# Attention denominators inverted in compact form once per four heads, with the heads passing DRAM and normalised four at a time

## The chip, the cores and the metric

The kernel runs on one core of a Trainium2 chip. The metric is the device time of one execution in microseconds. Five engines work side by side, each through its own instructions in order: TensorE (PE, with weight loads as PEld), VectorE (DVE), ScalarE (ACT), GpSimd (POOL) and SyncE (SP), which here issues every DMA.

## The reference

Two rows of 1024 tokens of width 512 pass six layers: half-weighted FFN 0, attention 0, FFN 0, FFN 1, attention 1, FFN 1, each behind a layer norm and added to its input. Only the attention layers are touched. Cut to the part that matters:

```python
att = jnp.einsum('bhqd,bhkd->bhqk', q, k) / scale      # 16 heads of 32, t = 1024, causal
att = jax.nn.softmax(att, axis=-1)
y = jnp.einsum('bhqt,bhtd->bhqd', att, v)
y = y.transpose(0, 2, 1, 3).reshape(b, t, n)
return y @ Wo.T + bo
```

The kernel leaves the softmax undivided until after the product with `v`: it computes a numerator `y` and a denominator per query, and multiplies by the inverse.

## The kernel before

`STAGES` lists the six layers; the attentions are stages 1 (`a0`, tiles `s1a0...`) and 4 (`a1`, tiles `s4a1...`). Each has 2 x 16 = 32 heads, worked in 8 groups of `HPG` = 4, groups 0 to 3 for the first batch row and 4 to 7 for the second. `make_plan` writes one list of steps and every engine's program walks it in that order, taking its own part of each step, so the list fixes the order on every engine and on SP's queue. Nothing overtakes.

A unit is one head and one key tile of 128: unit u is head u // 8, tile u % 8, and a group is 32 units. In unit u the plan puts, in this order: the steps due in jobs that run beside (`side.tick(0)`), the row maxima `row` for the unit 13 ahead (`AHEAD`: L1130 on PE, L1501 on DVE), the transposed scores `key` (L1148 on PE, exponentials L1335 on ACT), masking and pair sums on POOL (L1660, L1671), every second unit the products `pv` and `den` of units 9 back (L1167, L1178 on PE), and last the DMAs `stack` (L1745) that lay out q (and k) of the next group's heads: head 0's at unit 18 of the group, the others at 20, 26 and 31. The first `row` of the next group is in unit 19, and waits for head 0's stack. In attention 0 a k stack is needed once in four groups, in attention 1 in each.

PSUM holds for a head one bank of 128 x 512: on the partitions four quarters of the queries by 32 channels, in columns 0 to 255 the numerators, in columns 256 to 511 the denominators, each repeated over its 32 partitions. `times_v` starts a job when a head's last product is placed. For the last head of group g that is unit 7 of group g + 1, and the steps follow (units of group g + 1):

- 8: `y_fin`, on DVE a reciprocal of 128 x 256 (L1540) and a multiplication into `ysb` (L1544). It also frees the PSUM bank.
- 11: `y_move`, on SP four DMAs of 32 partitions (L1764) that bring the head from `ysb` into its 32 partitions of `y`.
- 14 and 15: `y_hi` (ACT, L1343) and `y_lo` (DVE, L1554), which split the group's `y` of 128 x 1024 into two parts in `yT`.
- 17 to 24: `oproj`, one token tile in each unit (PE, L1049), with `x_sum` (DVE, L1568) one unit behind.

The weights of the output projection of the next `oproj` come at unit 23 (`w_in`, SP) and are split at unit 24 on ACT (`w_split`, L1237) and POOL (L1635); the split waits for the last `oproj` of the group before, since it writes over its weights. Other weights of the next groups are loaded at units 17 and 19. `m_lo` (SP, L1755, units 5, 13, 21, 29) brings a head's maxima to its q stack, for its keys three units later. `bank_turns` gives the PSUM banks out by an estimate of when each comes free.

Of the kernel before, what the change touches and what calls it, by code (L numbers as in the profile page):

```python
# [17 lines left out]
P = 128  # L18
# [36 lines left out]
YT_AT = 2  # L55
O_LAG = 1
# [27 lines left out]
def into_heads(s):  # L84
    return s + 1 < len(STAGES) and not is_ffn(s + 1)

# [50 lines left out]
def make_plan():  # L137
# [112 lines left out]
    def attention(s, left):  # L250
# [71 lines left out]
        for g in range(GROUPS_ALL):  # L322
# [6 lines left out]
            put([split(s, "o", g, 0)], at + O_W_AT, 0)  # L329
# [18 lines left out]
        def times_v(n, jt):  # L348
# [5 lines left out]
            if k == PAIRS - 1:  # L354
                job = [[]] * Y_AT + [[("y_fin", s, n)]] + [[]] * Y_WAIT + [[("y_move", s, n)]]
                g, j = divmod(n, HPG)
                if j == HPG - 1:
                    job += [[]] * YT_AT + [[("y_hi", s, g)]] + [[("y_lo", s, g)]] + [[]] * O_LAG
                    job += timed(*((O_STEP * t, ("oproj", s, g, t)) for t in range(ST)),
                                 *((O_STEP * t + X_AFTER, ("x_sum", s, g, t)) for t in range(ST)))  # L360
                side.start(job)
# [65 lines left out]
    "e_add": ("e_add",), "den": ("den",), "y_fin": ("y_rec", "y_fin"),  # L427
# [59 lines left out]
class Pace:  # L487
# [10 lines left out]
    def run(self, step, banks):  # L498
# [84 lines left out]
        elif kind == "y_fin":  # L583
            done[step] = work("dve", 0.9, ("pv", s, where[0], ST - 1))
        elif kind == "y_hi":
            done[step] = work("act", 1.1, ("y_fin", s, (where[0] + 1) * HPG - 1))
# [9 lines left out]
def bank_turns(plan):  # L596
# [5 lines left out]
    for step in plan:  # L602
        width = banks_wanted(step)
        needs = []
        if width:
# [13 lines left out]
            if step[0] == "pv":  # L619
                release["y_fin", step[1], step[2]] = mine  # L620
# [44 lines left out]
def build(nc, a, out):  # L665
# [6 lines left out]
    with ExitStack() as ctx:  # L672
# [17 lines left out]
        moved = [ctx.enter_context(nc.semaphore(f"moved{i}")) for i in range(2)]  # L690
        stored = ctx.enter_context(nc.semaphore("stored"))
# [26 lines left out]
        for s, kind in enumerate(STAGES):  # L718
            t = T[s] = {}
            with ExitStack() as sc:  # L720
# [47 lines left out]
                else:  # L768
# [20 lines left out]
                    t["rden"] = [sbuf(sc, f"{tag}rden{i}", [P, QUAD]) for i in range(2)]  # L789
                    t["ysb"] = [sbuf(sc, f"{tag}ysb{i}", [P, QUAD]) for i in range(2)]  # L790
# [125 lines left out]

        def quarters_of(y):
            return y[:].rearrange("p (c t q) -> p t c q", c=HPG, q=HD)
# [49 lines left out]
        def read_by(step, k):  # L968

            kind = step[0]  # L970
            if kind == "pv":
                return sem["y_fin"], at("y_fin", "y_fin", *step[1:3])
# [225 lines left out]
        def scalar_program(act):  # L1198
# [138 lines left out]

            def y_hi(s, g):
                for n in range((g + 1) * HPG - 2, (g + 1) * HPG):
                    on.wait_ge(*y_moved(s, n))  # L1340
                if g:
                    on.wait_ge(sem["o_proj"], at("o_proj", "oproj", s, g - 1, ST - 1))
                act.activation(by_quarter(T[s]["yT"][HI]), quarters_of(T[s]["y"]),  # L1343
# [4 lines left out]
                     "key": key, "y_hi": y_hi}  # L1348
# [500 lines left out]
```

## Time and profile before

| | us |
|---|---|
| Median of three runs (lowest, highest) | 2633.96 (2629.57, 2639.21) |
| Span of the profiled execution | 2632.3 |
| PE busy in it | 2535.4 (96%) |
| DVE busy | 1533.2 (58%) |
| ACT busy | 1035.6 (39%) |
| POOL busy | 981.6 (37%) |

Attention 0 takes up about 320 to 780 us of the span, attention 1 about 1600 to 2095 us. The figures of whole engines mix these with four FFN layers, in which PE hardly ever rests, so the attentions are read by windows. Busy time on PE is modelled at the ends of its matmuls and can hide short waits.

### The profile page before, as it was taken

To read this page: it belongs to the slowest core of one execution; us is meant where nothing else is said; L and a number is where in the kernel's file an instruction comes from. 1 tells how busy PE (TensorE), PEld (TensorE's weight loads), DVE (VectorE), ACT (ScalarE), POOL (GpSimd) and SP (SyncE) were. 2 spreads that over 40 slices of the span, in tenths; PEclk is the share of its full clock that TensorE was granted. 3 is DMA by queue.
4 is the path that set the end of the run, shared out by engine and by line. 5 is a ranking of instruction groups with operands and counts; after the bars stand their busy time and mean duration, and the time that the engine had idled before them with its cause. 6 is when DMAs were issued, how large, how long until landed. Compare 5 with 4: busy or idle time off the path is not lost.

```text
span 2632.3 us, 44135 instructions
## 1 busy us (share of the span) xinstructions
PE 2535.4 (96%) x16928; PEld 2013.0 (76%) x16928; DVE 1533.2 (58%) x3356; ACT 1035.6 (39%) x1885; POOL 981.6 (37%) x1373
## 2 busy tenths in 40 slices
PE   6999989999999999999999999999999999999999
PEld 4788867667668888888888878677776678888887
DVE  7777579979975445433333345798589643333333
ACT  6555346656653223311111133566466431111111
POOL 5333566666643225211111122666366521111110
PEclk9999989999999999999999999999999999999999
DMA  4222131222220110100000002343233100000001
GB/s 148 73 73 73 39 76 46 51 68 64 48 93 1 36 45 12 37 25 25 24 25 25 25 17 58 92 94 75 52 88 79 37 32 25 24 25 25 25 17 64
DMA packets 72002, 128.73 MB, mean 49 GB/s; under 512 B 15728, under 2 KB 24944, under 8 KB 71792
## 3 DMA queue, kind: packets, MB, share of 16 engines
q1 hardware_dynamic: 71792, 125.92, 17.3%
q8 instruction: 134, 2.20, 0.4%
q14 instruction: 76, 0.62, 0.1%
HBM read 62.42 MB, written 13.63 MB: 29 GB/s over the span
## 4 chain that ended last, share of the span: by engine, by line
PE 81%; DVE 6%; POOL 2%; ACT 2%; SPq 2%; issue 2%; DMA 1%; DVEq 0%; ACTq 0%; POOLq 0%
PE psum L1049 65%; PE psum L1167 5%; PE psum L1130 4%; PE psum L1148 4%; PE psum L1178 2%; DVE psum L1501 2%; SPq L1745 1%; PE psum L1058 1%; DVE s1a0rden L1540 1%; ACT s1a0e L1335 1%; SPq L1764 0%; POOL s1a0e L1671 0%; ACT s4a1e L1335 0%; PE psum L1137 0%; POOL rstd L1610 0%
## 5 line engine op out<-in xcount | busy, mean ns | idle before, releaser
L1501 DVE CUSTOM_DVE_ANT_0 psum<-psum,mask_q 128x512 f32<-128x512 f32 (+5 forms) x768 | 413.2, 574 | 101.2 <-PE psum L1130 97.3
L1049 PE MATMUL psum<-hA_hi,wmem 128*128 128x256 f32 (+1 forms) x1536 | 405.2, 334 | 0.5 <-DVE s1a0negmax L1501 0.3
L1049 PEld LDWEIGHTS psum<-hA_hi,wmem 128*128 128x128 f32 x1536 | 270.3, 190 | 31.8 <-DVE s1a0negmax L1501 1.5
L1049 PE MATMUL psum<-hA_lo,wmem 128*128 128x512 f32 (+1 forms) x864 | 293.8, 340 | 0.0
L1335 ACT ACTIVATE s4a1e<-psum,p_scale 128x384 f32<-128x384 f32 (+5 forms) x384 | 205.5, 581 | 95.2 <-PE psum L1148 91.8
L1335 ACT ACTIVATE s1a0e<-psum,p_scale 128x384 f32<-128x384 f32 (+5 forms) x384 | 202.4, 578 | 78.1 <-PE psum L1148 76.8
L1454 DVE SCALAR_TENSOR_TENSOR x<-psum,x 128x512 f32<-128x512 f32 x256 | 175.7, 689 | 97.4 <-PE psum L1049 93.9
L1425 DVE TENSOR_TENSOR s5f1prod<-psum,s5f1silu 128x512 f32<-128x512 f32 x64 | 44.2, 691 | 303.7 <-PE psum L1049 303.7
L1425 DVE TENSOR_TENSOR s3f1prod<-psum,s3f1silu 128x512 f32<-128x512 f32 x64 | 44.2, 691 | 294.2 <-PE psum L1049 294.2
L1635 POOL TENSOR_TENSOR wmem<-raw,wmem 128x512 fp32r<-128x512 f32 x58 | 74.3, 1290 | 315.7 <-ACT wmem L1237 315.7
L1049 PE MATMUL psum<-s3f1w,s3f1a 128*128 128x512 f32 x768 | 181.6, 390 | 0.9 <-POOL s3f1w L1635 0.9
L1049 PE MATMUL psum<-s5f1w,s5f1a 128*128 128x512 f32 x768 | 180.0, 390 | 1.6 <-POOL s5f1w L1635 1.6
L1049 PEld LDWEIGHTS psum<-hA_lo,wmem 128*128 128x128 f32 x864 | 164.8, 191 | 19.8
L1671 POOL TENSOR_TENSOR s4a1e<-s4a1e 128x896 f32<-128x896 f32 (+3 forms) x128 | 164.8, 1288 | 17.4 <-ACT s4a1e L1335 6.4
L1671 POOL TENSOR_TENSOR s1a0e<-s1a0e 128x896 f32<-128x896 f32 (+3 forms) x128 | 164.6, 1286 | 17.1 <-ACT s1a0e L1335 5.8
L1049 PEld LDWEIGHTS psum<-s5f1w,s5f1a 128*128 128x128 f32 x768 | 143.9, 188 | 32.3 <-issue 2.0
L1049 PEld LDWEIGHTS psum<-s3f1w,s3f1a 128*128 128x128 f32 x768 | 143.5, 188 | 31.1 <-DVE s3f1prod L1425 1.1
L1645 POOL TENSOR_TENSOR x<-x,s0f0dso 128x512 f32<-128x512 f32 x64 | 89.0, 1412 | 136.1 <-DVE s0f0dso L1449 136.1
L1660 POOL TENSOR_SCALAR_AFFINE_SELECT s4a1e<-s4a1e 128x128 f32<-128x128 f32 x256 | 74.9, 299 | 166.6 <-ACT s4a1e L1335 164.9
L1635 POOL TENSOR_TENSOR s5f1w<-raw,s5f1w 128x512 fp32r<-128x512 f32 x32 | 40.8, 1296 | 242.4 <-ACT s5f1w L1237 242.4
L1635 POOL TENSOR_TENSOR s3f1w<-raw,s3f1w 128x512 fp32r<-128x512 f32 x32 | 40.8, 1295 | 241.4 <-ACT s3f1w L1237 241.4
L1148 PE MATMUL psum<-s1a0qst,s1a0kst 98*128 98x384 f32 (+4 forms) x384 | 118.1, 362 | 12.9 <-ACT s1a0e L1335 7.8
(195 smaller groups left out, 5581.8 us busy)
## 6 DMA issues: line engine op xcount, KB each, us to landing
s1a0qst<-s1a0qs SPq DMA_DIRECT2D x96, 128.0 KB, 2.3
s4a1qst<-s4a1qs SPq DMA_DIRECT2D x96, 128.0 KB, 2.4
s4a1kst<-s4a1ks SPq DMA_DIRECT2D x96, 128.0 KB, 2.4
raw<-in_gate SPq DMA_DIRECT2D x44, 256.0 KB, 2.9
raw<-in_up SPq DMA_DIRECT2D x44, 256.0 KB, 2.8
raw<-in_down SPq DMA_DIRECT2D x44, 256.0 KB, 2.8
rounded<-s0f0w SPq DMA_DIRECT2D x24, 256.0 KB, 2.0
s2f0w<-rounded SPq DMA_DIRECT2D x24, 256.0 KB, 4.9
```

The lines of the kernel that those rows point to most:

```text
L1049: ins = pe.matmul(out_, w, m, start=n == 0, stop=n == len(terms) - 1)
L1130: pe.matmul(ps[:, 0, 0:pw], q_st[0:STACK, j, i * P:(i + 1) * P], k_st[0:STACK, j, z * pw:(z + 1) * pw], start=True, stop=True).then_inc(se ...
L1148: pe.matmul(ps[:, 0, 0:pw], k_st[0:STACK + 2, j, jt * P:(jt + 1) * P], q_st[0:STACK + 2, j, q0 + z * pw:q0 + (z + 1) * pw], start=True, st ...
L1167: ins = pe.matmul(psum[c * HD:(c + 1) * HD, bank, jt * HD:QUAD], v[:, jt, kv, :], e[:, :, c, :], start=jt == 0, stop=jt == ST - 1, skip_gr ...
L1335: act.activation(T[s]["e32"][:, begin_ + z * pw:begin_ + (z + 1) * pw - skip], src, ACT.Exp, bias=p_scale[:]).then_inc(sem["exp"], 1)
L1425: dve.tensor_tensor(prod[:], psum[:, bank, :], silu[:], ALU.mult).then_inc(sem["prod"], 1)
L1454: dve.scalar_tensor_tensor(x[:, tile, :], src, 0.5, x[:, tile, :], ALU.mult, ALU.add).then_inc(sem["x_add"], 1)
L1501: dve.tensor_tensor_reduce(scores, scores, mask_q[:, first:first + pw], -1.0, -MASKED, ALU.add, ALU.min, T[s]["negmax"][n % 2][:, column:c ...
L1635: pool.tensor_tensor(lo, buf[:], hi.bitcast(F32), ALU.subtract).then_inc(sem["w_lo"], 1)
L1645: pool.tensor_tensor(x[:, tile, :], x[:, tile, :], T[s]["dso"][nth(*step) % 2][:], ALU.add).then_inc(sem["x_pool"], 1)
L1660: pool.affine_select(out=block, in_=block, compare_op=ALU.is_ge, fill=0.0, base=0, pattern=[[1, P]], channel_multiplier=-1).then_inc(sem[" ...
L1671: pool.tensor_tensor(e32[:, begin + P:end], e32[:, begin + P:end], e32[:, more:more_end], ALU.add).then_inc(sem["e_add"], 1)
```

## The change

For all groups but the last of each attention (`in_place`), the head is no longer inverted and multiplied in PSUM. ACT copies the whole bank of 128 x 512 into a larger `ysb` (`y_out`). One DMA stores it in DRAM (`y_save`, 256 KB), one loads the numerators back into `y` (`y_load`, 128 KB). Once in four heads, `den_in` reads the denominators without repetition, 4 x 1024 numbers laid out as 128 x 32; DVE inverts these (`y_rec`), `y_keep` stores them in DRAM, `y_spread` reads them back repeated over 32 partitions per head (128 x 1024, 512 KB) into `spread`, which shares memory with the high part of `yT`, and DVE multiplies the group's `y` by it (`y_norm`). The last group of each attention keeps the old way. The units of group g + 1 in which the steps stand:

| step | engine | before | after |
|---|---|---|---|
| y_fin / y_out | DVE / ACT | 8 | 8 |
| y_move / y_save | SP | 11 | 10 |
| y_load of heads 0 to 2 (ahead of y_save) | SP | - | 10 |
| y_load of head 3, den_in | SP | - | 13 |
| y_rec | DVE | - | 15 |
| y_keep | SP | - | 16 |
| y_spread | SP | - | 18 |
| y_norm | DVE | - | 22 |
| y_hi, y_lo | ACT, DVE | 14, 15 | 23, 24 |
| oproj | PE | 17 to 24 | 26 to 33 |
| x_sum | DVE | 18 to 25 | 27 to 34 |
| w_in, w_split of the next oproj | SP, ACT and POOL | 23, 24 | 35, 36 |

Units 33 and up lie in the next group. The heads' own `y_save` stand in units 2, 10, 18 and 26. Core of the diff:

```diff
+SAVE_WAIT = 1
+LOAD_WAIT = 2
+REC_AT, KEEP_AT, SPREAD_AT, NORM_AT = 2, 3, 5, 9
+def in_place(g):
+    return g == GROUPS_ALL - 1
...
-            put([split(s, "o", g, 0)], at + O_W_AT, 0)
+            if g == 0:
+                put([split(s, "o", g, 0)], at + O_W_AT, 0)
...
+                else:
+                    job = [[]] * Y_AT + [[("y_out", s, n)]] + [[]] * SAVE_WAIT
+                    job += [[("y_load", s, m) for m in range(n - j, n) if j == HPG - 1]
+                            + [("y_save", s, n)]]
+                    job += [[]] * LOAD_WAIT
                 if j == HPG - 1:
-                    job += [[]] * YT_AT + [[("y_hi", s, g)]] + [[("y_lo", s, g)]] + [[]] * O_LAG
+                    if not in_place(g):
+                        job += timed((0, ("y_load", s, n)), (0, ("den_in", s, g)),
+                                     (REC_AT, ("y_rec", s, g)), (KEEP_AT, ("y_keep", s, g)),
+                                     (SPREAD_AT, ("y_spread", s, g)), (NORM_AT, ("y_norm", s, g)))
+                    job += [[("y_hi", s, g)]] + [[("y_lo", s, g)]] + [[]] * O_LAG
...
+            def y_out(s, n):
+                if n >= 2:
+                    on.wait_ge(*ysb_left(s, n - 2))
+                on.wait_ge(sem["pv"], at("pv", "pv", s, n, ST - 1))
+                act.activation(T[s]["ysb"][n % 2][:], psum[:, banks["pv", s, n, 0][0], :],
+                               ACT.Copy).then_inc(sem["y_out"], 1)
...
+            def y_rec(s, g):
+                on.wait_ge(den_loaded, 16 * (nth("y_rec", s, g) + 1))
+                dve.reciprocal(T[s]["rden"][:], T[s]["den"][:]).then_inc(sem["y_rec"], 1)
+            def y_norm(s, g):
+                on.wait_ge(y_loaded, HPG * 16 * (nth("y_norm", s, g) + 1))
+                on.wait_ge(rden_spread, 16 * (nth("y_norm", s, g) + 1))
+                y = T[s]["y"]
+                dve.tensor_tensor(y[:], y[:], T[s]["spread"], ALU.mult).then_inc(sem["y_norm"], 1)
...
+            def y_load(s, n):
+                g, j = divmod(n, HPG)
+                on.wait_ge(*y_saved(s, n))
...
+            def y_keep(s, g):
+                k = nth("y_keep", s, g)
+                on.wait_ge(sem["y_rec"], at("y_rec", "y_rec", s, g))
...
+            def y_spread(s, g):
+                k = nth("y_spread", s, g)
+                on.wait_ge(rden_kept, 16 * (k + 1))
...
+                sp.dma_start(T[s]["spread"], rdens[k % 2].unsqueeze(1).broadcast_to([HPG, HD, SEQ])
+                             ).then_inc(rden_spread, 16)
```

## Rows read from the trace of the kernel before

**Rows 1.** Busy time by windows, both attentions (columns: PE, PEld, DVE, ACT, POOL, clock, DMA).

```profile
365.00:769.00 404.00, 378.49 (x4375) 274.38 (x4372) 356.17 (x985) 244.03 (x481) 282.73 (x445) 0.99 0.24 58
...
1645.00:2083.00 438.00, 417.62 (x4654) 313.87 (x4653) 355.13 (x972) 257.93 (x507) 271.86 (x436) 0.99 0.32 76
```

**Rows 2.** Same view, single groups, cut at unit 13: attention 0, then attention 1.

```profile
412.40:460.60 48.20, 46.97 (x557) 34.68 (x555) 45.46 (x129) 29.55 (x59) 32.65 (x51) 1.00 0.24 57
460.60:521.70 61.10, 55.16 (x601) 39.54 (x601) 56.40 (x156) 39.96 (x77) 42.57 (x75) 1.00 0.20 50
521.70:588.00 66.30, 60.23 (x626) 45.08 (x624) 50.85 (x138) 32.53 (x67) 43.94 (x60) 0.97 0.29 66
...
685.00:739.90 54.90, 49.59 (x542) 33.41 (x541) 51.31 (x146) 37.43 (x70) 39.81 (x74) 0.97 0.25 60
...
1696.00:1749.80 53.80, 52.65 (x606) 40.70 (x605) 47.21 (x132) 32.27 (x64) 33.29 (x52) 1.00 0.36 85
1749.80:1810.60 60.80, 56.71 (x626) 42.30 (x625) 54.33 (x151) 41.31 (x79) 42.37 (x76) 1.00 0.32 76
1810.60:1890.40 79.80, 76.66 (x714) 60.22 (x713) 47.23 (x135) 34.59 (x69) 33.38 (x52) 1.00 0.24 58
...
1997.20:2053.70 56.50, 52.30 (x566) 35.41 (x565) 53.45 (x147) 39.06 (x74) 41.31 (x75) 0.97 0.34 81
```

**Rows 3.** Chain of waits at unit 24 of group 1, attention 0 (start us, us, what).

```profile
430.53 0.37 ACT s1a0ow L1237
```

**Rows 4.** Groups of ACT instructions in attention 0, shapes apart.

```profile
L1229 ACT ACTIVATE hA_hi<-psum 128x512 fp32r<-128x512 f32 x16 | 9.5, 593 | 0.0
...
L1237 ACT ACTIVATE s1a0ow<-raw 128x512 fp32r<-128x512 f32 x8 | 5.1, 632 | 9.2 <-PE psum L1049 4.9 <-DMA raw<-in_o 4.3
```

**Rows 5.** Groups of DVE instructions, shapes apart: busy us, mean ns | idle before.

```profile
L1540 DVE RECIPROCAL s1a0rden<-psum 128x256 f32<-128x256 f32 x32 | 55.9, 1745 | 6.4 <-PE psum L1167 6.4
...
L1544 DVE TENSOR_TENSOR s1a0ysb<-psum,s1a0rden 128x256 f32<-128x256 f32 x32 | 13.6, 424 | 2.2
...
L1554 DVE TENSOR_TENSOR s1a0yT<-s1a0y,s1a0yT 128x1024 fp32r<-128x1024 f32 x8 | 9.9, 1234 | 1.6 <-ACT s1a0yT L1343 1.6
```

**Rows 6.** Timeline of ACT at a head's first unit, attention 0 [idle before <-releaser].

```profile
440.53 1.27 ACT L1335 ACTIVATE s1a0e<-psum,p_scale 128x512 f32<-128x512 f32 x2 [0.66 <-PE psum L1148]
```

**Rows 7.** Page, part 6: DMA issues, KB each, median us from issue to landing.

```profile
s1a0qst<-s1a0qs SPq DMA_DIRECT2D x96, 128.0 KB, 2.3
...
rounded<-s0f0w SPq DMA_DIRECT2D x24, 256.0 KB, 2.0
...
s1a0y<-s1a0ysb SPq DMA_DIRECT2D x128, 32.0 KB, 1.8
...
s1a0ropek<-in_rope SPq DMA_DIRECT2D x1, 512.0 KB, 4.2
```

**Rows 8.** Issues on SP of one line: min/median/max ns each.

```profile
L1745 SPq DMA_DIRECT2D s1a0qst<-s1a0qs x96: 507/590/1575, 324.6 to 721.6; - x96
```

**Rows 9.** Timeline, group 1 of attention 0, units 15 and 19 (start us, us, what).

```profile
414.06 0.62 PE L1130 MATMUL psum<-s1a0kst,s1a0qst 96*128 96x512 f32 x2
...
415.10 1.21 DVE L1554 TENSOR_TENSOR s1a0yT<-s1a0y,s1a0yT 128x1024 fp32r<-128x1024 f32 x1
...
421.21 0.40 PE L1130 MATMUL psum<-s1a0kst,s1a0qst 96*128 96x512 f32 x1
```

**Rows 10.** Timeline, group 0 of attention 0, the same rows, without output projections.

```profile
367.65 0.64 PE L1130 MATMUL psum<-s1a0kst,s1a0qst 96*128 96x512 f32 x2
...
372.63 0.40 PE L1130 MATMUL psum<-s1a0kst,s1a0qst 96*128 96x512 f32 x1
```

**Rows 11.** Timeline, group 1 of attention 1, units 15 and 19.

```profile
1700.38 1.22 DVE L1554 TENSOR_TENSOR s4a1yT<-s4a1y,s4a1yT 128x1024 fp32r<-128x1024 f32 x1
...
1700.81 0.63 PE L1130 MATMUL psum<-s4a1kst,s4a1qst 96*128 96x512 f32 x2
...
1708.10 0.47 PE L1130 MATMUL psum<-s4a1kst,s4a1qst 96*128 96x512 f32 x1 [0.56 <-DMA s4a1kst<-s4a1ks]
```

More of the change, by code:

```diff
@@ L583, in run @@
         elif kind == "y_fin":
-            done[step] = work("dve", 0.9, ("pv", s, where[0], ST - 1))
+            done["y", s, where[0]] = done[step] = work("dve", 2.2, ("pv", s, where[0], ST - 1))
+        elif kind == "y_out":
+            done["y", s, where[0]] = done[step] = work("act", 0.68, ("pv", s, where[0], ST - 1))
+        elif kind == "y_rec":
+            work("dve", 0.35)
+        elif kind == "y_norm":
+            work("dve", 1.25)
         elif kind == "y_hi":
-            done[step] = work("act", 1.1, ("y_fin", s, (where[0] + 1) * HPG - 1))
+            done[step] = work("act", 1.1, ("y", s, (where[0] + 1) * HPG - 1))
         elif kind == "y_lo":
@@ L690, in build @@
         moved = [ctx.enter_context(nc.semaphore(f"moved{i}")) for i in range(2)]
+        saved = [ctx.enter_context(nc.semaphore(f"saved{i}")) for i in range(2)]
+        y_loaded = ctx.enter_context(nc.semaphore("y_loaded"))
+        den_loaded = ctx.enter_context(nc.semaphore("den_loaded"))
+        rden_kept = ctx.enter_context(nc.semaphore("rden_kept"))
+        rden_spread = ctx.enter_context(nc.semaphore("rden_spread"))
+        heads_out = nc.dram_tensor("heads_out", (2, HPG, P, CH), F32, kind="Internal").ap()
+        rdens = nc.dram_tensor("rdens", (2, HPG, SEQ), F32, kind="Internal").ap()
         stored = ctx.enter_context(nc.semaphore("stored"))
@@ L915, in y_moved, with y_saved, ysb_left, y_whole @@
             return moved[n % 2], HPG * 16 * (nth("y_move", s, n) // 2 + 1)
+        def y_saved(s, n):
+            return saved[n % 2], 16 * (nth("y_save", s, n) // 2 + 1)
+        def ysb_left(s, n):
+            return y_moved(s, n) if in_place(n // HPG) else y_saved(s, n)
+        def y_whole(s, g):
+            if in_place(g):
+                return [y_moved(s, n) for n in range((g + 1) * HPG - 2, (g + 1) * HPG)]
+            return [(sem["y_norm"], at("y_norm", "y_norm", s, g))]
         def quarters_of(y):
@@ L971, in read_by @@
             if kind == "pv":
[L972 removed]
+                name = "y_fin" if in_place(step[2] // HPG) else "y_out"
+                return sem[name], at(name, name, *step[1:3])
             if kind == "piece":
@@ L1769, in sync_program @@
+            steps = {"begin": begin, "open": open_, "y_move": y_move, "y_save": y_save, "y_load": y_load, "den_in": den_in,
+                     "y_keep": y_keep, "y_spread": y_spread, "x_in": x_in_, "w_in": w_in, "w_keep": w_keep,
                      "w_back": w_back, "stack": stack, "m_lo": m_lo}
```

66 lines of the change are left out of this document (47 added, 19 removed).

## The prediction

> **What bounds the kernel now.** The busy times of the whole span mix the attentions with four FFN layers, so I cut the span at the attentions, the only layers touched, and read busy time by windows. In attention 0 PE is busy 378.5 of 404.0 us and DVE 356.2; in attention 1 it is 417.6 of 438.0 and 355.1 [rows 1]. PE therefore rests 25.5 + 20.4 = 45.9 us in both. That is the ceiling of any gain, since the change takes no matmul away, and it matters more than the DVE time that is saved.
>
> Next I cut by groups [rows 2]. Two kinds show. In an ordinary group PE rests 48.2 - 47.0 = 1.2 us (attention 0) or 53.8 - 52.7 = 1.1 us (attention 1); groups 4 and 5 repeat these. Groups 2 and 6 carry layer norms and group 3 the turn to the other batch row. There PE rests 5.9, 6.1 and 5.3 us in attention 0, and 4.1, 3.1 and 4.2 us in attention 1, together 28.7 us, with DVE at 56.4 of 61.1 and 51.3 of 54.9 us. So DVE limits three groups in eight; in the rest PE is full.
>
> The chain of waits tells what the 1.2 us of an ordinary group are. At unit 24 ACT splits the weights of the output projection only after the last projection of the group before; the exponentials behind it come late, and PE waits for a bank: 0.37 us of the split stands on the chain itself [rows 3], with an exponential behind it. ACT's idle time ahead of these splits, 4.9 us, has PE as releaser [rows 4].
>
> **DVE's part.** 56 of the 64 heads lose 1.745 + 0.424 = 2.17 us each [rows 5], 121.5 us. 14 groups gain a reciprocal of 32 columns instead of 256, 1.745 / 8 = 0.22 us (up to 0.3 with a start-up cost), and a product of 128 x 1024, for which the nearest row is the subtraction of that shape, 1.23 us [rows 5]. That is 14 x 1.5 = 21 us. DVE is relieved of 100 us, but PE gets back at most its rest. Of the 28.7 us in groups 2, 3 and 6 I take 60%, 17 us (between 8 and 26: ACT and the DMAs of these groups hold a part). In the six ordinary groups the split moves to unit 36, two units behind the last projection, which cures that wait: 6 x 1.1 = 6.5 us. Relief: 23.5 us, at most 35 us.
>
> **ACT's part.** 56 copies of a bank, 0.593 us each by the copy of that shape [rows 4], 33 us of ACT. ACT is busy 244 of 404 and 258 of 438 us [rows 1], so time is there, but the copy stands at unit 8 of each head's count, just ahead of the two longest exponentials, behind a wait for the head's last product. Queued behind it are the exponentials that free PE's banks. ACT rests 0.66 us at such a place now, waiting for PE [rows 6], and the bank of the head itself comes free 1.6 us earlier (0.6 instead of 2.17). I take 0.1 us a head, 5 us; the bounds are 0 (all in the gap, or a little below by the earlier bank) and 33 us.
>
> **SP's part, and the wait that is new.** Four issues a head become two, plus three a group; issues get fewer, yet three of the new ones wait for a DMA to land or for DVE, and SP's queue stands still behind them. I follow which waiter matters.
>
> `y_load` and `den_in` wait for `y_save` to land. From the end of the last product: 0.6 copy, 2.0 store (the 256 KB store [rows 7]), two issues, about 2.2 for the load: 6 us. `y_rec` is seven units later, 8.7 us at PE's pace of 5.0 us for four units [rows 10] (these are the heavy units, so rather less). It is just in time, and the maxima of unit 13 behind it on SP aren't due before. I cost this at nothing; if the cover goes, DVE waits and all below moves out by the same time.
>
> The pair `y_keep`, `y_spread` is another matter. `y_spread` stands in unit 18 and a unit's jobs come ahead of its stacks. So the q stack of the next group's first head, in unit 18 too, and PE's first `row` on it, unit 19, stand behind: DVE reaching `y_rec`, its end, the landing of `y_keep`, the issue of `y_spread`, the issue of `y_save`, and only then the stack's own issues and landing. PE is in order, so everything waits with that `row`.
>
> In time, for attention 0: `y_rec` stands where `y_lo` stood, 415.10 in group 1 [rows 9]. Then 0.3 (reciprocal) + 1.9 (between 1.8 of the small DMA and 2.0 of a store to DRAM [rows 7]) + 0.5 + 0.5 (two issues at the shortest [rows 8]) + 1.2 + 2.3 (two more issues at the median [rows 8], and the landing of the stack's third from its issue [rows 7]) = 6.7 us, so the stack is there at 421.8. When does PE want it? Before, at 421.21, but three output projections lay between, and they now stand from unit 26 on. Group 0 has no projections and shows PE's own pace: 372.63 - 367.65 = 5.0 us from the `row` of unit 15 to that of unit 19 [rows 10]. From 414.06 [rows 9] this gives 419.1. Stall: 2.7 us. In attention 1 a k stack follows, three issues or 1.8 us more: 1700.38 + 8.5 = 1708.9, wanted at 1700.81 + 5.0 = 1705.8 [rows 11]; the stall is 3.1 us. The wait of 0.56 us that is there now [rows 11] goes off it: 2.5 us.
>
> To this comes that the 512 KB of `y_spread` and the 256 KB of `y_save` travel just ahead of the stack. A 512 KB load took 4.2 us against 2.3 for 128 KB [rows 7]. The surplus of 1.9 us is a bound, as most of it runs while SP still issues; I take 0.9 us. So 3.6 and 3.4 us, or 3.5 in each ordinary group: 6 x 3.5 = 21 us. In groups 2, 3 and 6 of both attentions the stall falls partly into rest that is there anyway, and I take half: 6 x 1.75 = 10.5 us. Group 0 has no `y_spread` in it, group 7 no stack. Sum 31.5 us. Bounds: 12 x 0 if something else holds PE or DVE reaches unit 15 much sooner, 12 x (3.1 + 1.9) = 60 us.
>
> Where a page bears on it: the rows show 1.8 to 2.0 us for DMAs of 32 KB as of 256 KB [rows 7]. The Trainium skill, "DMA: Bandwidth & Descriptors", in its anatomy of one DMA, puts a fixed cost of some 2.0 us on each and says that it is mostly the receipt of the write, which can take long when the target is HBM. With that 2.0 for each landing, `y_keep` costs 0.1 us more, 12 x 0.1 = 1 us. The same page asks for pieces of 512 bytes or more; `den_in` and `y_keep` move pieces of 128 bytes, and no row before shows a store of this kind. The trace agrees as to the fixed cost.
>
> **Late projections.** They fill units 26 to 33 instead of 17 to 24. PE's work is the same. The groups' q and k pieces lie in units 0 to 14, so only the last two projections meet them. At the end of a stage the projection of group 6 runs out of the loop by two tiles, and the last group's weights follow it while the last head is still inverted and moved; I cost that at nothing, 1 us a stage if not covered.
>
> **Sum.** 31.5 + 5 - 23.5 = +13 us. Against the span of the profiled execution, 2632.3 us, which is 1.7 us under the median of the runs and well inside their spread, this is 2645.3, rounded to 2645 us.
>
> **Rivals.**
>
> - The stack is not late (faster). If DVE, freed of its backlog, reaches `y_rec` a unit or two earlier relative to PE, or PE is slowed in units 15 to 19 by the copies on ACT so that it doesn't want the stack sooner, the stall is gone and only relief is left: 2632.3 - 23.5 + 5 = 2614 us, down to 2600 with the upper relief. Against it: DVE's slot in group 0 and 1 lies just one microsecond behind PE's `row`, so there is hardly a backlog to lose; for it, that in groups 2 and 6 DVE does lag.
> - Both cancel (same). Stalls at half my size, 16 us, or relief of 35 us: 2632.3 + 16 + 5 - 23.5 = 2630 us, to 2636.
> - ACT becomes the limit at head starts (slower still). With 0.6 us per head on PE's path, 33 instead of 5 us: 2645 + 28 = 2673 us. It decides from the point where ACT's rest ahead of unit 8 is below the copy; the idle time of ACT at large speaks against it.
> - The change doesn't do what it says: if the loads kept DVE waiting at `y_rec` or `y_norm`, DVE would stand while its rows are due and lose what it was given; 14 groups x 2 us on top of the forecast give 2673 us. Part of the slower case.
>
> **How the numbers follow.** The forecast, between 2638 and 2660, has 0.45. The faster rival has 0.22, the cancelling one 0.23, the two worse ones together 0.10. A measurement of this kernel can tell about 0.3% or 8 us from no change, 2626 to 2642. Of the forecast's 0.45 some 0.07 lie under 2642, and the upper edge of the faster rival and the lower of the cancelling one meet at 2626. So faster 0.21, same 0.31, slower 0.48. The range leaves out the lower half of the faster rival and the worst of the slow ones: 2614 to 2668 us.
>
> **What would show it.** In the changed profile, the `row` instructions of PE (scores for the maxima) that follow a new stack should wait 3 us for the DMA of the q stack in attention 0 and the k stack in attention 1, twelve times, 30 us or more in sum. On SP the q stack should start right behind `y_spread`, some 3 us after the small reciprocal. DVE should be busy about 100 us less over both attentions, and ACT 33 us more. The wait of the output weights' split for the projection should be gone. The prediction is wrong if these `row` waits sum to under 15 us, or if PE's rest in groups 2, 3 and 6 shrinks by much more than 17 us.

## The result and the profile after

The changed kernel takes 2800.7 us in the median (2798.2 to 2802.1) against 2636.6 for the kernel before beside it. The ratio is 1.0626, with a 95% interval of 1.0607 to 1.0645: 164 us slower, where 13 had been forecast. The sign was right, the size was wrong by a factor of twelve, and the time lies far outside the range of 2614 to 2668 us.

The head of the page of the kernel after (span; busy time and share of each engine):

```profile
span 2798.2 us, 43919 instructions
...
PE 2567.1 (92%) x16928; PEld 2034.9 (73%) x16928; DVE 1466.8 (52%) x3272; ACT 1059.9 (38%) x1941; POOL 995.5 (36%) x1373
```

Two sums can be read from it. PE rests 2798.2 - 2567.1 = 231.1 us, and 2632.3 - 2535.4 = 96.9 before, so 134.2 us more. And PE is busy 31.7 us longer with the same 16928 matmuls. The two make up the whole difference of the spans, 165.9 us. The second one says that the same matmuls took longer.

Who makes PE rest stands in the waits of PE (who waited for what: us in total, times, longest). L1182 is `row` (L1130 before), L1200 is `key`:

```profile
PE psum L1182 <- DMA s4a1kst<-s4a1ks: 78.5, 7, 13.8
PE psum L1182 <- DMA s1a0qst<-s1a0qs: 49.1, 5, 11.9
...
PE psum L1200 <- DMA s1a0qst<-s1a0mrow: 13.9, 4, 10.3
PE psum L1182 <- DMA s1a0kst<-s1a0ks: 13.7, 2, 11.6
PE psum L1200 <- DMA s4a1qst<-s4a1mrow: 10.3, 3, 9.6
```

The first row of scores of a group waits for its stack 14 times, 78.5 + 49.1 + 13.7 = 141.3 us. Two of these stacks have no broadcast ahead of them (2.1 and 3.4 us). The other twelve are the place which the prediction named: 135.8 us, or 11.3 us a time, where 3.5 us in an ordinary group and 31.5 us in all had been forecast. None of the twelve is under 8.2 us, so the half that the prediction took off in groups 2, 3 and 6 isn't there either. The two `mrow` lines (a head's maxima on their way into its q stack) have a single wait of some 10 us in each attention, which was not foreseen at all.

One such wait, group 1 of attention 0. SyncE's timeline there (start, us, line, transfer):

```profile
415.35 0.35 SPq L1864 DMA_DIRECT2D rdens<-s1a0den  x1
415.75 0.43 SPq L1789 DMA_DIRECT2D raw<-in_q  x1
416.80 0.59 SPq L1872 DMA_DIRECT2D s1a0yT<-rdens  x1
417.45 0.46 SPq L1839 DMA_DIRECT2D heads_out<-s1a0ysb  x1
418.02 3.74 SPq L1811 DMA_DIRECT2D s1a0qst<-s1a0qs  x6
```

and the chain of waits through it:

```profile
415.12 0.22 DVE s1a0den L1607
415.35 1.43 DMA rdens<-s1a0den
416.80 0.59 SPq L1872
...
417.45 0.46 SPq L1839
...
419.27 9.05 DMA s1a0qst<-s1a0qs
...
428.46 0.77 PE psum L1182
```

The order and the times of the issues are those of the prediction almost to the tenth: `y_rec` at 415.12 (predicted 415.10), the stack's second issue ended at 419.2 (419.5 by the forecast). Then the landing takes 9.05 us instead of 2.3.

Why, the busy time by windows shows (us; PE, PEld, DVE, ACT, POOL; then the granted clock, the share of the 16 DMA engines that is busy, GB/s):

```profile
418.00:420.00 2.00, 0.70 (x3) 0.38 (x3) 1.58 (x3) 1.37 (x4) 1.82 (x1) 1.00 0.79 237
420.00:422.00 2.00, 0.00 (x0) 0.00 (x0) 0.28 (x1) 0.30 (x1) 1.73 (x3) 1.00 1.00 213
422.00:424.00 2.00, 0.00 (x0) 0.00 (x0) 0.00 (x0) 0.00 (x0) 0.00 (x0) 0.73 0.68 129
424.00:426.00 2.00, 0.00 (x0) 0.00 (x0) 0.00 (x0) 0.00 (x0) 0.00 (x0) 0.50 0.25 100
426.00:428.00 2.00, 0.00 (x0) 0.00 (x0) 0.00 (x0) 0.00 (x0) 0.00 (x0) 0.50 0.26 98
428.00:430.00 2.00, 1.54 (x7) 1.03 (x11) 0.63 (x2) 0.41 (x1) 0.00 (x0) 0.50 0.05 14
430.00:432.00 2.00, 2.00 (x26) 1.13 (x19) 0.13 (x2) 0.53 (x2) 1.67 (x2) 0.50 0.00 0
```

Two things are to be seen. From 424 to 428 a quarter of the DMA engines is busy, 4 of 16, at 100 GB/s. Under way are the broadcast `y_spread`, issued 7 us before, and the last parts of the stack; I read this as the broadcast on four engines, with the stack's share queued behind it, and test it below. And the granted clock: it is 1.00 while PE begins to rest, falls to 0.50 (1.2 of 2.4 GHz), and stays there until 432 at least, so PE's first microseconds of work after the rest run at half speed. The first `row` at 428.46 takes 0.77 us; before, at the full clock, it took 0.40 [rows 9]. That is where the same matmuls take longer.

Single instructions took about what was forecast. The `y_norm` takes 1.21 and 1.32 us (forecast 1.23), the small reciprocal 0.34 (0.22 to 0.3). The wait of the output weights' split for the projection, 4.9 and 5.0 us before, is gone. The copy on ScalarE, from the groups of ACT by shape, takes what the row of its shape said [rows 4]:

```profile
L1394 ACT ACTIVATE s1a0ysb<-psum 128x512 f32<-128x512 f32 x28 | 16.6, 593 | 1.8 <-PE psum L1219 1.6
```

But VectorE is busy only 66 us less over the span, where 100 had been forecast. 23 of the 34 missing stand in 64 small instructions that the change doesn't touch, the minima of 128 x 4 (L1510 before, L1569 after): 35.6 us before, 58.7 after. One of them, from the timelines of VectorE and GpSimd:

```profile
384.85 2.05 DVE L1569 TENSOR_TENSOR s1a0negmax<-s1a0negmax 128x4 f32<-128x4 f32 x1
384.79 2.09 POOL L1737 TENSOR_TENSOR s1a0e<-s1a0e 128x896 f32<-128x896 f32 x1
```

Alone such an instruction takes 0.16 us. Each one that takes more than 0.4 us, 29 of 64 before and 52 after, began while a GpSimd TENSOR_TENSOR was under way and ended within 0.04 us of its end. So VectorE stands there until GpSimd is done, and after the change it comes to that place more often while GpSimd works. Part of the relief is lost that way.

### The profile page after: what moved, and what is told of

Read it like the earlier page. It is cut to its first block, busy times and chain, and to the rows that moved or that the text cites. A ratio compares the mean times of both kernels' runs of the same rounds, so it can differ in the third digit from the quotient of the medians.

```text
span 2798.2 us, 43919 instructions
## 1 busy us (share of the span) xinstructions
PE 2567.1 (92%) x16928; PEld 2034.9 (73%) x16928; DVE 1466.8 (52%) x3272; ACT 1059.9 (38%) x1941; POOL 995.5 (36%) x1373
## 4 chain that ended last, share of the span: by engine, by line
PE 80%; DMA 6%; DVE 4%; SPq 2%; issue 1%; ACT 1%; POOL 1%; DVEq 0%; ACTq 0%; POOLq 0%
PE psum L1101 63%; PE psum L1182 5%; PE psum L1219 5%; PE psum L1200 4%; DMA s4a1kst<-s4a1ks 2%; PE psum L1230 2%; DMA s1a0qst<-s1a0qs 2%; DVE psum L1560 1%; SPq L1811 1%; PE psum L1110 1%; DMA s1a0kst<-s1a0ks 0%; PE psum L1189 0%; DMA rdens<-s4a1den 0%; DMA rdens<-s1a0den 0%; DVE stats L1426 0%
## 5 line engine op out<-in xcount | busy, mean ns | idle before, releaser
L1182 PE MATMUL psum<-s4a1kst,s4a1qst 96*128 96x512 f32 (+4 forms) x384 | 127.3, 390 | 79.6 <-DMA s4a1kst<-s4a1ks 78.5
L1182 PE MATMUL psum<-s1a0kst,s1a0qst 96*128 96x512 f32 (+4 forms) x384 | 129.1, 396 | 63.8 <-DMA s1a0qst<-s1a0qs 49.1
L1737 POOL TENSOR_TENSOR s4a1e<-s4a1e 128x896 f32<-128x896 f32 (+3 forms) x128 | 166.3, 1300 | 17.4 <-ACT s4a1e L1387 6.5
L1726 POOL TENSOR_SCALAR_AFFINE_SELECT s4a1e<-s4a1e 128x128 f32<-128x128 f32 x256 | 81.2, 320 | 244.0 <-ACT s4a1e L1387 242.9
L1726 POOL TENSOR_SCALAR_AFFINE_SELECT s1a0e<-s1a0e 128x128 f32<-128x128 f32 x256 | 82.0, 325 | 176.8 <-ACT s1a0e L1387 176.4
L1182 PEld LDWEIGHTS psum<-s4a1kst,s4a1qst 96*128 96x128 f32 x384 | 68.9, 199 | 102.8 <-issue 86.0
```

The costliest lines, as they stand in the source:

```text
L1182: pe.matmul(ps[:, 0, 0:pw], q_st[0:STACK, j, i * P:(i + 1) * P], k_st[0:STACK, j, z * pw:(z + 1) * pw], start=True, stop=True).then_inc(se ...
L1726: pool.affine_select(out=block, in_=block, compare_op=ALU.is_ge, fill=0.0, base=0, pattern=[[1, P]], channel_multiplier=-1).then_inc(sem[" ...
L1737: pool.tensor_tensor(e32[:, begin + P:end], e32[:, begin + P:end], e32[:, more:more_end], ALU.add).then_inc(sem["e_add"], 1)
```

## Experiments on the broadcast

The kernel before took 2636.1 to 2639.3 us beside them, so medians can be compared directly, but between experiments that were run at different times only to about 3 us. The interval in brackets is that of the ratio to the kernel before.

**The broadcast as four DMAs.** Its source is 4 heads x 32 repetitions x 1024. The experiment issues one DMA by head, whose outermost dimension is 32:

```diff
-sp.dma_start(T[s]["spread"], rdens[k % 2].unsqueeze(1).broadcast_to([HPG, HD, SEQ]))
+for j in range(HPG):
+    sp.dma_start(T[s]["spread"][j * HD:(j + 1) * HD, :],
+                 rdens[k % 2, j].unsqueeze(0).broadcast_to([HD, SEQ]))
```

> The changed kernel with one edit: the DMA that spreads the inverses over the partitions is issued as four DMAs of 32 partitions, so that the outermost dimension of each is 32 and not 4. Its place in the queue stays. Theory A (width): in the changed kernel the spread's 512 KB went over a quarter of the 16 DMA engines (busy share 0.25 and 0.26 from 424 to 428 us, 100 GB/s), and the stack behind it on these engines landed 9 us late. Spread over all engines it is gone in 2 to 3 us; the wait of PE's row for the stack shrinks from 8 to 12 us to about 3 or 4 us each, 141 us to about 45 us in sum, and the kernel takes 2640 to 2665 us. Theory B (place): the wait comes from the order alone (inversion, store, landing, spread, stack), whatever the width; then 2790 us or more remain. Theory C: reading one DRAM row 32 times is what is slow; then it stays above 2750 us too, with the busy share high on all 16 engines.

Measured: 2719.1 us (1.0284 to 1.0318), 82 us less. Windows at the same wait, after a first issue of the broadcast at 414.64:

```profile
416.00:418.00 2.00, 0.55 (x3) 0.23 (x2) 1.73 (x3) 1.51 (x3) 1.96 (x1) 1.00 0.85 247
418.00:420.00 2.00, 0.00 (x0) 0.00 (x0) 0.14 (x1) 0.06 (x1) 1.59 (x3) 0.85 0.86 263
420.00:422.00 2.00, 0.65 (x2) 0.59 (x3) 0.00 (x0) 0.00 (x0) 0.00 (x0) 0.50 0.93 209
422.00:424.00 2.00, 2.00 (x23) 1.18 (x25) 0.76 (x2) 0.95 (x2) 0.78 (x2) 0.50 0.15 31
```

The stretch at a quarter is gone, and with it theories B and C. The first rows of the groups wait 65.4 us for stacks instead of 141.3. The width was half of the loss, but theory A had 2640 to 2665 us and about 45 us of waits: 2719 is well above it, and the rest has other causes. The four DMAs also add three issues ahead of the stack: its first issue comes 3.73 us behind that of `y_keep`, and 2.64 in the changed kernel (medians of twelve groups). So by width alone the loss is rather more than 82 us.

**The broadcast behind the first stack** (`SPREAD_AT` 5 to 6; one DMA), and **both edits together**:

> The changed kernel with one edit: the spread, still one DMA, stands in unit 19 and so behind the stack of head 0 (unit 18) and ahead of the k weights and the stack of head 1 (unit 20). Theory A (width): stack 0 is no longer behind the slow transfer, but the stack of head 1 and the maxima of unit 21 are; head 1's row is only due at unit 27, some 8 us later, so most of the 9 us is covered. The row's wait for stack 0 all but goes (under 2 us each), about half of the 164 us or more comes back: 2640 to 2700 us. Theory B (place): with the spread out of the way the time falls to about that of the kernel before or below, 2620 to 2640 us, and splitting it in four on top adds nothing.

> Both edits: four DMAs, in unit 19. My sum had 31.5 us for the stalls at stack 0, 23.5 us of relief and 5 us for the copies on ACT. Without the stall 2614 us are to come out (2605 to 2630). If the relief of DVE and of the weights' split is worth nothing, 2637 us; if the copies on ACT cost 33 us, 2640 us or more. Against e1 the difference is the price of the place alone, once the width is cured: 20 to 40 us.

Measured: 2743.6 (1.0381 to 1.0415) and 2689.5 us (1.0171 to 1.0201). Both expectations were missed: theory A had 2640 to 2700 us for the first, and 2605 to 2630 had been expected of the second. The difference to the first experiment, 20 to 40 us by expectation, was met: the place ahead of the stack costs 30 us with the wide broadcast (57 with the narrow one). The width still costs 54 us where the broadcast stands behind the stack: `key` then waits for the maxima (18.3 and 10.9 us), and in attention 1 `row` waits for ScalarE's exponentials, 20.6 us in four waits, which I have not followed further.

**One DMA, but with an outermost dimension of 16.** The first experiment leaves open whether four DMAs help by being four. Here the reciprocals are kept four times over, so that one DMA can read 16 rows, each 8 times:

```diff
-rdens[k % 2].unsqueeze(1).broadcast_to([HPG, HD, SEQ])
+rdens[k % 2].rearrange("j r q -> (j r) q").unsqueeze(1).broadcast_to([HPG * HPG, HD // HPG, SEQ])
```

> The changed kernel (2800.7), the broadcast still one DMA of 512 KB to the same places, but the reciprocals are kept four times over, so that the outermost dimension of its source is 16 and not 4 (three small stores more by group). Theory (the outermost dimension of 4 leaves 12 of the 16 DMA engines out, and the stacks queue behind on the four): as with four DMAs of 32 partitions (2719), 2705 to 2730, and the stretch at a quarter of the DMA engines is gone. Rival (one DMA of 512 KB is slow by its size or by reading the same 4 KB again and again, and four DMAs were quicker for being four): 2785 or more.

Measured: 2752.0 us (1.0413 to 1.0453), between the two, and a miss: 2705 to 2730 had been expected. The trace shows both halves of that. Windows, then SyncE's timeline:

```profile
422.00:424.00 2.00, 0.00 (x0) 0.00 (x0) 0.00 (x0) 1.15 (x3) 1.51 (x2) 0.50 0.95 272
424.00:426.00 2.00, 0.00 (x0) 0.00 (x0) 0.00 (x0) 0.00 (x0) 0.00 (x0) 0.50 1.00 336
```

```profile
415.84 2.64 SPq L1865 DMA_DIRECT2D rdens<-s1a0den  x4
418.54 0.47 SPq L1789 DMA_DIRECT2D raw<-in_q  x1
419.91 0.61 SPq L1873 DMA_DIRECT2D s1a0yT<-rdens  x1
420.56 0.58 SPq L1839 DMA_DIRECT2D heads_out<-s1a0ysb  x1
421.25 3.77 SPq L1811 DMA_DIRECT2D s1a0qst<-s1a0qs  x6
```

All 16 engines are busy, at 336 GB/s (broadcast and stack together), no stretch at a quarter follows, and the one DMA lands in 4.9 us (median). So the outermost dimension is the cause, not the number of DMAs.

Why it isn't 2719: the four small stores occupy SyncE for 2.64 us instead of 0.35, so the stack's first issue comes 5.0 us behind that of the first store (median of twelve groups). With four broadcasts it is 3.73. The number of issues ahead of the stack is the same there, one store and four broadcasts against four stores and one broadcast, but those of the broadcasts are shorter (0.4 us against 0.55). That is 1.3 us a group, some 15 of the 33 us. The stack also lands later behind the one DMA, in 4.12 us instead of 3.04 in this group. Together the first rows wait 94.4 us for stacks instead of 65.4, 29 of the 33 us. My expectation had left these issues out.

The rule of the width could have been read beforehand. The Trainium skill, "DMA: Bandwidth & Descriptors", section "Why a DMA increments its semaphore by 16 and not by 1", says that a DMA runs on the largest number of engines up to 16 that divides the slowest dimension not of size 1 of its source and of its destination alike; for 4 and 128 that is 4. The trace agrees: 0.25 of the engines.

**No keep, no spread.** `y` is multiplied by itself, which leaves the normalisation out and its VectorE time in:

> The changed kernel without the store of the inverses and without their spread; the group's y is multiplied by itself at the same place, so that the output is not normalised. DVE and ACT do the same work as in the changed kernel, SP waits for no landing ahead of the stack, and 512 KB per group are not moved. It is the floor of what the change can give. By my terms 2614 us; by the theory that all of the loss is the spread, 2636 us or less; if the copies on ACT, the stores of the heads or the late projections cost much by themselves, it stays above 2650 us.

Measured: 2676.6 us (1.0127 to 1.0157). So keep and spread, wide and behind the stack, cost 13 us. Without them the kernel is still 1.4% slower than before, where my terms had 2614 us: something other than the inverses' way is wrong too.

## Experiments on VectorE's relief and the late projections

**The weights' split later, in the kernel before** (`O_W_AT` 23 to 26):

> The kernel before with one number changed: the split of the next group's output weights lies at unit 26 of a group instead of 23, so VectorE no longer stands waiting at it while the projection of the units before runs. This is one term of my sum by itself (the wait in front of the split, 6.5 us over the twelve groups, which I took as given back to TensorE). If the term is right: about 2633 against 2639.3. If VectorE's wait was off TensorE's path: 2639, within 2. If the split then comes too late for the projection that uses it, TensorE waits there and the time rises over 2645.

Measured: 2641.3 (1.0003 to 1.0022). Nothing is gained, against the 6 us of the expectation. PE's waits for the exponentials are 9.4 + 9.4 us in it, against 7.8 + 8.3 before. The expectation speaks of VectorE where the split is on ScalarE and GpSimd; the number is unaffected.

**The kernel before without the reciprocal, and then with ScalarE's copy in place of the whole normalisation.** In the second nothing of it is left on VectorE. Both leave out the true normalisation, and both change all 64 heads:

```diff
-dve.reciprocal(rden[:], psum[:, bank, QUAD:CH])
-dve.tensor_tensor(T[s]["ysb"][n % 2][:], psum[:, bank, 0:QUAD], rden[:], ALU.mult)
+act.activation(T[s]["ysb"][n % 2][:], psum[:, banks["pv", s, n, 0][0], :], ACT.Copy)
```

> The kernel before without the 56 reciprocals: the numerators are multiplied by ones, so the normalisation is left out, and the 1.7 us by head that the change wants to save are gone with nothing put in their place: no DMA, no copy by ScalarE, no later projection. It measures the relief of VectorE alone. My theory (it was the limit only in stretches of groups 2, 3 and 6): 17 us less, about 2622. Rival (VectorE was nowhere the limit, TensorE's share of 92% sets the time): within 3 of 2639. Second rival (it was the limit in every group): 2600 or less.

> The kernel before with the numerators leaving PSUM by a copy of ScalarE (128x512, numerators and denominators in one, as in the change) and nothing put on VectorE in its place; the normalisation is left out, the heads still go from chip to chip and the projections stay in their units. Against the kernel that left out the reciprocals alone (2628.7) it measures ScalarE's copy. My term: 5 us of TensorE's time, so about 2634 (bounds 0 to 33: 2629 to 2662). If the copy is what remains of the change when the spread is gone and the projections are back (2657), 2650 or more.

Measured: 2628.7 (0.9956 to 0.9980) and 2623.4 us (0.9934 to 0.9959). Taking the reciprocal away brings 7 to 8 us, where 17 had been expected. (The first expectation speaks of 56 reciprocals and of TensorE's share of 92%; the edit takes out 64, and 92% is the share in the changed kernel, 96% in the one before.) Taking the multiplication too and giving ScalarE the copy brings 5 more, where the copy was to cost 5. What the copy costs by itself isn't separated by this. The net relief is 14 us; 23.5 - 5 = 18.5 had been put down. It is what the change could have won if the inverses' way and the later order of work had cost nothing, and no run here was faster.

**The kernel before with late projections.** The halves of `y` nine units later, the split of the next output weights behind the projections, and the first head of a group moved behind the halves, so that SyncE doesn't stand there. Core of the edit:

```diff
-YT_AT = 2
+YT_AT = 11
-job = [[]] * Y_AT + [[("y_fin", s, n)]] + [[]] * Y_WAIT + [[("y_move", s, n)]]
+job = [[]] * Y_AT + [[("y_fin", s, n)]] + [[]] * (8 if g and j == 0 else Y_WAIT) + [[("y_move", s, n)]]
```

> The kernel before with the split of y and the projections later by nine units (y's two halves at units 22 and 23, the first projection at 25), the split of the next output weights behind them, and the first head of a group moved at unit 24, behind the halves, so that SyncE's queue doesn't stand there. Nothing else is changed: it is the step that I costed at nothing. Theory (the projections are the work that lies between the stacks' issue and the row of scores that reads them, and without them TensorE rests there and its clock falls): waits for the stacks grow from 8 to 30 us or more, 2655 to 2670. If my step was right: within 5 of 2636.

Measured: 2651.4 (1.0043 to 1.0071), 14 us more. PE's waits in it (L1133 is `row`):

```profile
PE psum L1133 <- DMA s4a1kst<-s4a1ks: 11.7, 7, 3.2
...
PE psum L1133 <- DMA s1a0kst<-s1a0ks: 6.2, 2, 4.0
```

They were 3.8 and 4.5 us before, so the projections did cover a part of the stacks' way. Moving them isn't free, as the prediction had it, and isn't the 19 us or more that I then expected of it.

> The kernel before with ScalarE's copy in place of the normalisation (2623.4) and with the late projections (2651.4) in one; the normalisation is left out. If the two terms are independent, 2637 (14 less, 14 more). If VectorE's relief is worth more where the projections are late, under 2633. The distance from here to the kernel without spread and with the saves behind the stacks is the price of the trips through DRAM themselves: I expect 0 to 6 us.

Measured: 2631.5 (0.9963 to 0.9985). Beside the copy on ScalarE, lateness costs 8 us and not 14. The terms aren't independent. The waits for the stacks are nearly the same (16.1 us against 17.9), and VectorE's share of the chain that ended last falls from 10% to 4%, so the gain is on VectorE's side; more than that isn't shown.

## Experiments on what was still open

**The tied head.** In group 7 heads go from `ysb` to `y` directly, as before. The first one's `y_move` (unit 19) overwrites `y`, so it waits for `y_lo` of group 6, which stood at unit 15 and now stands at 24. SyncE stands still at it, with the low half of the maxima queued behind. In the kernel with both edits (four DMAs, behind the stack), end of attention 0, the chain (L1613 is `y_norm`, L1402 and L1620 the halves, L1830 `y_move`, L1821 the maxima):

```profile
758.71 1.71 DVE s1a0y L1613
760.45 1.06 ACT s1a0yT L1402
761.53 1.46 DVE s1a0yT L1620
763.05 0.57 SPq L1830
...
765.57 0.69 SPq L1821
766.30 1.76 DMA s1a0qst<-s1a0mrow
768.20 1.94 PE psum L1200 x4
```

The experiment is the kernel with both edits and `Y_WAIT` 8 for that head alone:

> The kernel with the spread in four pieces and behind the first stack of the row (2689.5), with one number changed: in the group whose heads are moved to their place on the chip alone, the first head is moved at unit 25 and not at unit 19, so that SyncE's queue no longer stands at that move until the group before has been split into its two halves (unit 24), with the low half of the rotated keys queued behind. If the tie is what TensorE waits for at unit 24 of group 7 (8.1 us in each attention): 17 us less, about 2672. If the wait there has another cause, within 3 of 2689.

Measured: 2672.1 us (1.0123 to 1.0149), 17 less, as expected (13 by the ratios to the kernel before). The waits of `key` for the maxima were 10.9 and 9.2 us; 2.9 and 1.7 us are left. The maxima now go ahead of the moves:

```profile
761.78 1.32 SPq L1821 DMA_DIRECT2D s1a0qst<-s1a0mrow  x2
...
766.35 5.90 SPq L1830 DMA_DIRECT2D s1a0y<-s1a0ysb  x8
```

**Projections back in their units, without keep and spread** (`LOAD_WAIT` 2 to 0, `REC_AT` 1, `NORM_AT` 2):

> The kernel without the keep, the spread and the true reciprocals (the rows of y are multiplied by themselves; 2676.6), with the split of y and the projections back in the units in which the kernel before has them (14 to 24, instead of 23 on); loads and normalisation are moved earlier for it. Theory: the late projections no longer lie between the stacks' issue and the row of scores that reads them, and this costs some 30 us, and the tie at unit 24 of group 7 17 more, partly the same time: about 2620 to 2640. Rival (what is left over the kernel before comes from ScalarE's copies and the extra transfers): 2665 to 2680.

Measured: 2657.3 (1.0064 to 1.0091), 19 less than without that edit, of which the tie alone would be 17. Neither 2620 to 2640 nor the rival's 2665 to 2680 came out, and it was a poor experiment: it moved loads, product and projections at once, and PE waited 5.3 us in each attention for ScalarE's copies instead. It suggested, no more, that the late projections weren't what kept the time high.

**The saves ahead of the stacks.** The chain of the kernel without keep and spread, group 1 of attention 1:

```profile
1713.66 0.61 ACT s4a1ysb L1393
...
1714.29 0.34 SPq L1837
...
1714.74 0.56 SPq L1809
...
1719.37 2.40 DMA s4a1kst<-s4a1ks
...
1721.90 0.77 PE psum L1181
```

`y_save` (L1837) of the new group's first head stands one unit earlier than the `y_move` that it replaces, and thereby ahead of the stack and not behind it. It waits for ScalarE's copy, and the copy for the last product of the head. SyncE was done with the weights' load before it at 1709.14 + 0.44, and the stack's first issue comes at 1714.74, 5.2 us later. The experiment moves the saves of heads 0 and 1 one unit on, with the tied head moved later as well, once with the broadcast in four behind the stack, once without it:

```diff
-job = [[]] * Y_AT + [[("y_out", s, n)]] + [[]] * SAVE_WAIT
+job = [[]] * Y_AT + [[("y_out", s, n)]] + [[]] * (2 if j < 2 else SAVE_WAIT)
```

> The kernel with the broadcast in four, behind the stacks, and the tied head moved later (2672.1), with the saves of the first two heads of a group one unit later, so that they stand behind the stacks of units 18 and 26 in SyncE's queue and no longer ahead. Theory (the stacks wait behind a save that waits for ScalarE's copy): 15 to 22 us less, 2650 to 2657. Rival (the save costs nothing there, and what is left is the trips' traffic or the broadcast): within 4 of 2672.

> The kernel without keep, spread and true normalisation (2676.6), with the tied head moved later and the saves of the first two heads of a group behind the stacks. The tie alone gives 2659; with the saves' place right: 2637 to 2643. Rival (the saves cost nothing there): 2656 to 2662.

Measured: 2658.8 (1.0065 to 1.0099), 13 less than 2672.1 and a little short of the 15 to 22 expected, and 2639.9 us (1.0003 to 1.0026), 19 to 20 less than 2676.6 - 17.4 = 2659.2, as expected. SyncE's timeline without the broadcast:

```profile
1689.40 0.44 SPq L1787 DMA_DIRECT2D raw<-in_q  x1
1690.99 1.82 SPq L1809 DMA_DIRECT2D s4a1qst<-s4a1qs  x3
1694.73 2.32 SPq L1809 DMA_DIRECT2D s4a1kst<-s4a1ks  x3
1697.10 0.58 SPq L1837 DMA_DIRECT2D heads_out<-s4a1ysb  x1
```

The stack starts 1.2 us after the weights' load. Of the 22 us by which 2659.2 was over the kernel before, 19 are found. Between the late projections with ScalarE's copy (2631.5) and this kernel (2639.9) the trips through DRAM, the product of 128 x 1024, the small reciprocal and the old way of group 7 are left: 8 us, where 0 to 6 had been expected.

**All three mended, with one DMA whose source is 16 wide.**

> The changed kernel with all three mended: the source of the broadcast 16 wide, the broadcast behind the first stacks, and the first head of the last group moved at unit 25. It is the best form of the change in its own order of work. Sum of the single steps: 2672, as with four DMAs and the move later (2672.1); 2662 to 2682. If the steps don't add up so with one DMA, over 2690. By what is left (late projections, trips through DRAM, ScalarE's copy) it doesn't come below 2655, over the kernel before.

Measured: 2699.6 us (1.0217 to 1.0245), 27 over the same kernel with four DMAs and over the expected 2662 to 2682. The four stores hold the first stack up by 1.45 us a group in the mean, 17 us in twelve groups, and the first rows wait 66.7 us for stacks instead of 46.5; the rest of the 27 isn't shown. None of the versions with the whole normalisation beats the kernel before. The best, with the saves behind the stacks, is 0.8% over it: the relief is worth 14 us, and in every form tried the rest of the way through DRAM costs more than that.

## Why the prediction was wrong, step by step

The step that failed most is the 0.9 us a group (1.9 as its bound) that the prediction took for the bytes of `y_spread` and `y_save` ahead of the stack: the stack's landing took 9.05 us instead of 2.3. It had the place and the order right, and took the cost of the broadcast from its bytes. The late projections, put at nothing, cost 8 us; the tied head, which the prediction doesn't have, cost 17; and the issue of `y_save` was counted without the wait in it, 19.

One edit at a time, from the kernel before to the kernel after (each step is the difference of two medians, in this order; another order would share them out differently):

| step | us | predicted |
|---|---|---|
| the copy on ScalarE in place of the normalisation | -14 | -18.5 |
| projections and split late | +8 | 0 |
| trips through DRAM, product, small reciprocal | +8 | within the relief |
| saves ahead of the stacks (19 to 20) and the tied head (17) | +37 | 0.5 us a group for the save's issue; none for the tie |
| keep and spread, wide, behind the first stack | +13 | no term of its own |
| spread ahead of that stack | +30 | with the next, 31.5 |
| its width: 4 DMA engines instead of 16 | +82 | 0.9 us a group |

The steps of 8 us are known to about 3. The last row also holds what three fewer issues ahead of the stack give back; by 1.1 us a group, an estimate from the issue times above, the width alone would be some 95 us.

- *DVE's part and ACT's part* were of the right kind. The ceiling of PE's rest [rows 1, 2] held. The 6.5 us for the split [rows 3] were wrong: a wait that stands on the chain for 0.37 us is no proof that the time comes back when it goes (2641.3 us with the split later). VectorE was relieved of 66 us and not of 100; 23 of the missing 34 are the minima that stand behind GpSimd. ACT's term of 5 us doesn't show: the copy in place of the multiplication brought 5 us.
- *The wait that is new* was the right mechanism at the right place, and its issue times were right. PE wanted the stack when predicted too: it stops between 418 and 420, with 419.1 forecast. The term that failed is the surplus of 0.9 us for the 512 KB and 256 KB ahead of it, with 1.9 as a bound: the landing grew from 2.3 to 9.05 us. The bound came from a 512 KB load [rows 7] that has as many bytes but not the same pattern, and the pattern stood in the diff. The landing of `y_keep`, on the other hand, was put too long: 1.9 us in the sum, and it took 1.4 us (median). The 2.0 us that the prediction gives beside it are in the Trainium skill, "DMA: Bandwidth & Descriptors", anatomy of one DMA, those of DMAs that GpSimd issues; SyncE issues these.
- *The issue of `y_save`* was counted at 0.5 us, with its own condition, ScalarE's copy, left out. Moving the saves behind the stacks gave back 19 to 20 us without keep and broadcast, and 13 with both in place. In the changed kernel itself, with the broadcast ahead of the stack, it was not tried.
- *"PE's work is the same"* for the late projections was wrong because they were cover. The prediction used in its own stall that they no longer lie between units 15 and 19, and costed their absence at nothing everywhere else.
- *The tie* in group 7 was missed: of the steps moved later, only their own work was costed, not who waits for them. `y_lo` had a waiter on SyncE's queue.
- *The clock* was in no term. Of the 165.9 us, 31.7 are matmuls that took longer. The last column is PE's busy time in stretches of 2 us, each times what its granted clock lacked to 1.00, summed up:

| kernel | span | PE's rest | PE busy | busy x missing clock |
|---|---|---|---|---|
| before | 2632.3 | 96.9 | 2535.4 | 18.3 |
| saves behind, no spread | 2633.9 | 89.7 | 2544.2 | 27.6 |
| both edits (four, behind) | 2684.9 | 129.3 | 2555.6 | 40.9 |
| four DMAs | 2716.2 | 152.9 | 2563.3 | 49.4 |
| one DMA, behind | 2743.5 | 165.4 | 2578.1 | 69.0 |
| after | 2798.2 | 231.1 | 2567.1 | 55.8 |

The busy time grows by 9 to 43 us over the kernel before and the last column by 9 to 51, in the same order, so the longer matmuls are those under a lower clock. Both follow the sum of the rests only roughly: with one DMA behind the stack PE rests less than in the kernel after and works longer.

The rivals: the stack was late, so the faster rival fell. ACT was not the limit: `key` waited 5.8 us for ScalarE, and 16.1 before. VectorE waited for the spread ahead of `y_norm`, as the last rival has it, but only 2.8 + 1.2 us in all. The signs of being wrong that the prediction named were a wait of `row` under 15 us in sum, and a rest that shrinks too much. For 141.3 us it had no sign.

## What to carry to other kernels

Cost a new DMA by its pattern, not its bytes alone: look at the outermost dimension of both sides. The broadcast over 4 rows ran on 4 engines, and the transfers behind it landed late. In a queue that is worked in order, list what stands ahead of the one transfer that the busiest engine waits for, each with its own condition, and for each step that is moved later, who waits for it. And a rest of the bounding engine costs more than its length when its clock falls with it.

## What the runs showed of the hardware

- The broadcast of 512 KB with an outermost dimension of 4 kept a quarter of the DMA engines busy at 100 GB/s. With 16 no such stretch was left: all engines were busy, at 336 GB/s with the stack beside it, and it landed in 4.9 us (median).
- The granted clock was 1.00 in the first two microseconds in which PE did nothing, 0.73 in the next two, then 0.50. PE began to work again at 428.46 us, and it was still 0.50 from 430 to 432.
- An instruction of VectorE on 128 x 4 numbers took 0.16 us alone and up to 2.05 us when a GpSimd instruction of 2.09 us was under way, and ended with it.
- A store of 16 KB in pieces of 128 bytes to DRAM landed in 1.4 us in the median, less than any store of the kernel before [rows 7]. The load of the denominators, also 16 KB, took 2.2 to 2.3.
- Left open: of the stack issues in the kernel without keep and spread one took 2.09 us instead of 0.59 (chain of waits at 1715.34 us), and nothing in the trace says why.
